# Chunk 0's gates ahead of the last attention units' closing steps, with a new place for the zero fills, the weight splits and TensorE's branch

## The reference

```python
x = x + _L0_xattn_ref(_layernorm(x), ctx, ctx, ...)   # layer norms on q, k, v, softmax, Wo; a sigmoid gate and a layer norm close it
x = x + _L0_ffn_ref(_layernorm(x), ...)               # silu(x w1) * (x w2), then gelu(h h1), gelu(h h2), h w3; ternary weights
x = x + _L1_xattn_ref(_layernorm(x), ctx, ctx, ...)   # softmax attention, w_o
x = x + _L1_ffn_ref(_layernorm(x), ...)               # relu(x W1 + b1) W2 + b2
```

## Time and profile before

| | us |
| --- | --- |
| median of 3 runs | 988.79 (988.23 to 990.15) |
| the profiled execution | 985.62 |
| its span, first to last instruction | 983.7 |
| TensorE busy | 932.3 (95%) |
| ScalarE busy | 776.5 (79%) |
| VectorE busy | 705.6 (72%) |
| GpSimd busy | 364.8 (37%) |
| mean granted TensorE clock | 0.992 |

### The profile page before, as it was taken

The page is one execution under the profiler, slowest core; times in us unless marked ns, Lnnn a source line. Parts: engine busy times, 40 slices in busy tenths (PEclk is TensorE's granted clock), DMA queues, the critical chain, the costliest instruction groups (busy, mean ns, idle before and its releaser), DMA issues.

```text
span 983.7 us, 33064 instructions
## 1 busy us (share of the span) xinstructions
PE 932.3 (95%) x12363; PEld 722.0 (73%) x12363; DVE 705.6 (72%) x1918; ACT 776.5 (79%) x1537; POOL 364.8 (37%) x546
## 2 busy tenths in 40 slices
PE   5999999999969999999999999799999999889998
PEld 3677777877658888887888887557777777558886
DVE  8789889887766666666766665366766766478985
ACT  3688888888768988888888887468878888659886
POOL 6989999997420000000000000254444443011110
PEclk9999999999999999999999999899999999999999
DMA  6333322211000000000000000022222221000111
GB/s 204 97 95 97 99 72 83 74 44 39 6 0 1 1 0 0 0 0 0 0 0 0 0 0 22 31 80 75 65 64 65 71 65 55 17 2 33 43 39 58
DMA packets 46550, 41.75 MB, mean 42 GB/s; under 512 B 24400, under 2 KB 32592, under 8 KB 46416
## 3 DMA queue, kind: packets, MB, share of 16 engines
q1 hardware_dynamic: 45408, 37.26, 12.3%
q10 hardware_dynamic: 1008, 2.64, 0.8%
HBM read 16.79 MB, written 4.19 MB: 21 GB/s over the span
## 4 chain that ended last, share of the span: by engine, by line
PE 78%; ACT 8%; DVE 6%; issue 6%; DMA 1%; POOL 0%; ACTq 0%; SPq 0%; DVEq 0%; POOLq 0%
PE ps_w L1046 15%; PE ps_w L1045 15%; PE ps_av L578 6%; PE ps_w L528 5%; ACT prob_t L671 3%; PE ps_w L525 3%; PE ps_w L511 3%; PE ps_mid L600 3%; PE ps_mid L601 3%; PE ps_turn L588 2%; PE ps_turn L615 2%; PE ps_mid L643 2%; PE p_ps_out L1044 2%; ACT v_by_head L742 2%; PE p_ps_out L1046 1%
## 5 line engine op out<-in xcount | busy, mean ns | idle before, releaser
L848 DVE TENSOR_REDUCE top<-ps_w 128x16 f32<-128x1024 f32 x128 | 155.7, 1217 | 76.6 <-PE ps_w L525 76.1
L1045 PE MATMUL ps_w<-g_h_lo,w_hi 128*128 128x512 f32 x512 | 206.1, 402 | 3.9 <-DVE g_h_lo L1266 3.9
L1046 PE MATMUL ps_w<-g_h_hi,w_hi 128*128 128x512 f32 x512 | 203.1, 397 | 0.0
L1266 DVE TENSOR_TENSOR g_h_lo<-g_h,g_h_hi 128x512 fp32r<-128x512 f32 x192 | 133.0, 693 | 91.3 <-ACT g_h_hi L1215 87.4
L133 POOL TENSOR_TENSOR front_rstd<-front_spread,minus_half 128x4 f32<-128x4 f32 x33 | 34.3, 1041 | 416.7 <-DVE front_spread L126 416.7
L525 PE MATMUL ps_w<-qk_sets,qk_t 32*64 32x256 f32 x2048 | 142.4, 387 | 0.0
L1215 ACT ACTIVATE g_h_hi<-g_h 128x512 fp32r<-128x512 f32 x192 | 121.3, 632 | 21.6 <-DVE g_h L1276 17.6
L528 PE MATMUL ps_w<-qk_sets,qk_t 32*64 32x256 f32 x2048 | 133.7, 375 | 0.8 <-issue 0.8
L671 ACT ACTIVATE prob_t<-ps_w 128x1024 f32<-128x1024 f32 x128 | 130.5, 1020 | 4.7 <-PE ps_w L528 4.5
L1045 PEld LDWEIGHTS ps_w<-g_h_lo,w_hi 128*128 128x128 f32 x512 | 96.8, 189 | 26.1 <-DVE g_h_lo L1266 4.1
L1046 PEld LDWEIGHTS ps_w<-g_h_hi,w_hi 128*128 128x128 f32 x512 | 97.0, 189 | 21.8
(11 more groups left out here) (160 smaller groups left out, 2107.4 us busy)
## 6 DMA issues: line engine op xcount, KB each, us to landing
qk_sets<-qk_t SPq DMA_DIRECT2D x256, 64.0 KB, 1.9
ctx_in<-in_ctx SPq DMA_DIRECT2D x32, 128.0 KB, 2.8
ctx_in<-in_ctx_t SPq DMA_DIRECT2D x32, 128.0 KB, 2.6
out_x<-x_res SPq DMA_DIRECT2D x16, 256.0 KB, 2.0
x_res<-in_x SPq DMA_DIRECT2D x14, 256.0 KB, 3.4
shift<-pieces SPq DMA_DIRECT2D x128, 16.0 KB, 2.3
w_raw<-in_ff_weights SPq DMA_DIRECT2D x8, 256.0 KB, 3.3
w_raw<-in_ff_weights ACTq DMA_DIRECT2D x1, 768.0 KB, 8.0
```

The lines of the kernel that those rows point to most:

```text
L848: nc.vector.tensor_reduce(out=top[:, i % 2, half, :], in_=bank_pair(half).rearrange("p (a q) -> p a q", q=SEQ), op=ALU.max, axis=AX.X).the ...
L1045: nc.tensor.matmul(out, w_hi, x_lo, start=first and w_lo is None, stop=False)
L1046: return nc.tensor.matmul(out, w_hi, x_hi, start=False, stop=last)
L1266: nc.vector.tensor_tensor(h_lo[level][:, o, :], h[:, o % 2, :], h_hi[level][:, o, :].bitcast(F32), ALU.subtract).then_inc(lo_ready[level], 1)
```

## The change

It has five parts.

1. The zero fills leave GpSimd. ScalarE fills `qk_sets` slots 0 and 1 and `v_by_head` slots 2 and 3 before its first copy, and `qk_sets` slots 2 and 3 at step -1, by copying the bf16 zeros of `blank`. VectorE's fill of `v_by_head` slots 0 and 1 moves behind unit 0's statistics. A new semaphore, `slots_cleared`, counts ScalarE's fills.
2. The four scatters of unit 0 are shared: two by SP, two by ScalarE's queue, right behind `qk_t` of unit 0.
3. `split_weights_hi` moves, in ScalarE's step, from its end to the place between `top_parts` and `top_t`.
4. VectorE's steps N+3 and N+4 of the first attention move into the gated stage: chunk 0's products first, then `front_normalise` of chunk 1 and step N+3; step N+4 ahead of chunk 1's products. For chunk 0 TensorE takes `middle(0, 1)` by quarters, waiting for one quarter at a time in its first output quarter, with the transposes of chunk 1 behind it; ScalarE's copy of these transposes follows the first gelu.
5. TensorE's three later stages are functions that are called inside both sides of the branch, so the side without low products runs on into the second attention.

The core of the diff:

```diff
@@ open_scalar
     nc.scalar.activation(t.qk_bias[:, 1, 0:1], t.cols[:, COLS["b_q"]:COLS["b_q"] + 1], ACT.Copy, scale=float(HEAD_DIM) ** -0.5)
+    act.wait_ge(op.zeros_ready, op.BLANK)
+    clear_operands(nc, t, op, slice(0, FIRST_SLOTS))
+    clear_values(nc, t, op, slice(FIRST_SLOTS, UNROLL))
@@ open_gpsimd
-    nc.gpsimd.memset(t.qk_sets[:, 0:FIRST_SLOTS, :, :, :], 0.0).then_inc(op.zeros_ready, 1)
...
-def open_late_zeros(nc, t, op):
-    late = slice(FIRST_SLOTS, UNROLL)
-    nc.gpsimd.memset(t.v_by_head[:, late, :, :], 0.0)
-    nc.gpsimd.memset(t.qk_sets[:, late, :, :, :], 0.0).then_inc(op.zeros_ready, 1)
+def clear_operands(nc, t, op, slots):
+    wide = t.qk_sets[:, slots, :, :, :].rearrange("p s m n u -> p (s m) (n u)")
+    nc.scalar.activation(wide, t.blank[:, :].unsqueeze(1).to_broadcast([P, FIRST_SLOTS * SETS, 512]), ACT.Copy).then_inc(op.slots_cleared, 1)
+
+
+def clear_values(nc, t, op, slots):
+    wide = t.v_by_head[:, slots, :, :].rearrange("p s h c -> p s (h c)")
+    width = UNIT_TILES * HEADS * PAIR_COLS
+    for s in range(FIRST_SLOTS):
+        last = nc.scalar.activation(wide[:, s, :].rearrange("p (a n) -> p a n", n=512),
+                                    t.blank[:, :].unsqueeze(1).to_broadcast([P, width // 512, 512]), ACT.Copy)
+    last.then_inc(op.slots_cleared, 1)
@@ open_values
-    nc.vector.memset(t.v_by_head[:, 0:FIRST_SLOTS, :, :], 0.0).then_inc(op.chain, 1)
@@ open_weights
     nc.vector.tensor_copy(t.qk_bias[:, 1, 1:2], c["b_k"])
+    nc.vector.memset(t.v_by_head[:, 0:FIRST_SLOTS, :, :], 0.0).then_inc(op.chain, 1)
     dve.wait_ge(op.bias_done, 1)
@@ attention, scalar step
                     last.then_inc(qk_taken, 1)
+                if i == 0:
+                    act.wait_ge(qk_taken, 1)
+                    scatter(act, 0, range(SETS // 2, SETS))
                 if j < 0:
                     take_turned(j + 3)
+                if gated and j == -1:
+                    clear_operands(nc, t, op, slice(FIRST_SLOTS, UNROLL))
...
                     nc.scalar.activation(top_parts[:, j % 2, :, :, :], each_part, ACT.Copy).then_inc(top_split, 1)
+                split_weights_hi(nc, t, t.opening, act, layer, j)
                 if on(j):
                     act.wait_ge(top_turned, j + 1)
...
                 if j >= 0:
                     take_turned(j + 3)
-                split_weights_hi(nc, t, t.opening, act, layer, j)
@@ attention, vector
-                if j == N + 3:
+                if not gated and j == N + 3:
                     front_normalise(nc, t, front, dve, 1, front.slots - 1)
...
-            for j in range(-5, N + 5):
+            t.first_attention_step = step
+            for j in range(-5, N + 3 if gated else N + 5):
@@ gated_feed_forward, tensor: middle and step
+            def middle(i, level, between=None):
...
+                by_quarter = isinstance(i, int) and (i == 0 if level == 1 else i + 1 >= N)
+                if not by_quarter:
+                    wait(pe, lo_ready[level - 1], 4 * i + 4)
...
+                        if by_quarter and o == 0:
+                            wait(pe, lo_ready[level - 1], 4 * i + c + 1)
...
+                    if o == 0 and between is not None:
+                        between()
...
+                if opening(j):
+                    middle(j, 1, between=turn_next)
+                else:
+                    turn_next()
                     middle(j, 1)
@@ gated_feed_forward, vector step
+                if opening(j):
+                    split_lo(j, 1, 0)
                 if ahead(j + 1):
                     front_split_in(nc, t, front, dve, j + 1, 0, ps_in[:, :])
...
+                if opening(j):
+                    t.first_attention_step(t.tiles // UNIT_TILES + 4)
                 product_stage(j + 1)
+                if opening(j + 1):
+                    front_normalise(nc, t, front, dve, 1, 0)
+                    t.first_attention_step(t.tiles // UNIT_TILES + 3)
                 residual(j - 1)
@@ two_layer_xattn_ffn
+            @block.tensor
+            def _(pe):
+                with pe.If(t.lows_absent):
+                    t.gated_stage(pe, with_lo=False)
+                    t.second_attention(pe)
+                    t.plain_stage(pe)
+                with pe.Else():
+                    t.gated_stage(pe, with_lo=True)
+                    t.second_attention(pe)
+                    t.plain_stage(pe)
```

More of the change, by code:

```diff
@@ L494, in attention, with scatter, tensor_program @@
         closing_row = t.ln_o_b[:, :] if gated else t.bias_row[:, 1, :]
+        def scatter(queue, i, sets):
+            s = i % UNROLL
+            for m in sets:
+                queue.dma_start(qk_sets[m:P:SETS, s, m, :, :], qk_t[m:P:SETS, i % QKT, :, :]).then_inc(qk_landed[s], 16)
         def bank_pair(half):
             return ps_w[:, half * 1024:(half + 1) * 1024]
-        @block.tensor
-        def _(pe):
+        def tensor_program(pe):
             def half_step(turned_unit, turned_half, unit, half):
@@ L664, in _ @@
                     t.lows_absent = pe.value_load(t.lo_bits_row[0:1, 0:1].bitcast(I32))
+        if gated:
+            block.tensor(tensor_program)
+        else:
+            t.second_attention = tensor_program
         @block.scalar
@@ L839, in _ @@
                 step(j)
-                if gated and j == -2:
-                    open_late_zeros(nc, t, op)
         @block.vector
@@ L1070, in following, with opening @@
         return isinstance(i, int) and i == N
+    def opening(j):
+        return isinstance(j, int) and j == 0
     LEVELS = 3
@@ L1186, in _, with hidden @@
-            with pe.If(t.lows_absent):
-                program(with_lo=False)
-            with pe.Else():
-                program(with_lo=True)
+                up(j + 1, (0, 1))
+                down(j - 1)
+                up(j + 1, (2, 3))
+                turn_back(j - 1)
+                middle(j, 2)
+            steps.run(pe, step)
+        t.gated_stage = tensor_program
         @block.scalar
         def _(act):
-            def hidden(i, level):
+            def hidden(i, level, between=None):
@@ L1196, in hidden @@
                 for o in range(4):
+                    if o == 1 and between is not None:
+                        between()
                     wait(act, done[level], 4 * i + o + 1)
@@ L1245, in step, with take_next @@
             def step(j, u):
-                if ahead(j + 1):
-                    front_take_in(nc, t, front, act, j + 1, 0, ps_in[:, :])
-                hidden(j, 1)
+                def take_next():
+                    if ahead(j + 1):
+                        front_take_in(nc, t, front, act, j + 1, 0, ps_in[:, :])
+                if opening(j):
+                    hidden(j, 1, between=take_next)
+                else:
+                    take_next()
+                    hidden(j, 1)
                 silu_stage(j + 1, after=j - 1)
@@ L1293, in step @@
                     front_measure(nc, t, front, dve, N, 0, chunk=0)
-                if on(j):
+                if on(j) and not opening(j):
                     split_lo(j, 1, 0)
```

132 lines of the change are left out of this document (61 added, 71 removed).

## The result

The changed kernel takes 975.3 us (median of four runs, 972.8 to 975.7) against 989.5 for the one before (median of four beside it, 988.2 to 991.2): a ratio of 0.985, 95% interval 0.983 to 0.986. A second series gave 973.8 against 987.5, ratio 0.986 (0.983 to 0.989). So the gain is 14.2 and 13.7 us where 13.8 was forecast.

The account below looks back on a forecast made before the run. TensorE carries 78% of the chain, so only its standstills can move. Savings of 1.7 + 3.1 + 1.0 + 4.2 + 3.8 = 13.8 us take the median from 988.8 to 975.0, range 972 to 978.

Parts of the forecast that it names:

- The opening: Start of the kernel: zero fills off GpSimd let the first values come sooner, 1.7 us gained, from -1 to 3.
- The splits: Attention steps with a weight split: the earlier w_hi copy gains 3.1 us in the first attention, 1.0 in the second.
- the allowance of 0.15 us for each split: First attention's six split steps: 0.9 us in all left as cost, taking the gain from 4.0 to 3.1.
- The first border: First attention to gated stage: first product 2.9 us earlier, level 1 ending 5.4 or 3.8 earlier, 4.2 taken.
- The wait for `front_normalise`: First border: TensorE's transposes of chunk 1 wait from two matmuls' end at 276.5 until 277.05, a new wait.
- The second border: Gated stage to second attention: without the jump's 3.09 us wait qk_t starts 3.9 us earlier, 3.8 kept.
- The next wants (unit 2's normed rows, 628.5) are met: Second border: what TensorE needs after the earlier first products is ready in time, so 3.8 us is kept.
- The jump at the end: End of TensorE's program: a 3.1 us jump ends at 983.5, inside the span; counted as nothing, 0.5 at most.
- Rival B: Second border: the wait is not the jump's, or returns as another; gain 10.0 us, time 978.8; chance 0.12.
- C: Attention: ScalarE bounds the steps, so moving its 0.63 us copy gains nothing; time 979.1; chance 0.10.
- D: Opening gives nothing, ScalarE's fills and queue issue eating VectorE's gain; -1 instead of 1.7, time 977.7; chance 0.08.
- E: ScalarE's fills run below a third of the expected pace and eat the 13.8 us gain; time 991; chance 0.02.

Follow-up runs that it names:

- split_at_end: The changed kernel with part 3 undone, the copy to w_hi back at the end of ScalarE's step: 978.9 us.
- warm: Zero matmuls added in TensorE's waits at both borders, against the kernel with shared scatters behind ScalarE's copy of transposes: 968.3 us, ratio 0.980.
- jump: The changed kernel with part 5 undone, the branch closing behind the gated stage: 979.2 us, ratio 0.991.
- fills_gpsimd: The changed kernel with ScalarE's three zero fills back on GpSimd: 975.9 us, ratio 0.988.

## Why the prediction was right, point by point

**The opening, 1.7 forecast.** The two pairs of profiles give 1.05 and 1.7 at the same row. The mechanism is the one named: `halves` at 0.39 us, ScalarE's fills hidden, the first values at 22.91 (22.5 forecast). The fills' pace was 0.88 to 0.97 ns a column for 0.8, so the fills ahead of the first copy ended at 11.65 instead of 11.1; 0.54 us of slack was left only because the first copy came at 12.20 instead of 11.8. VectorE's own fill takes 1.76 us with no fill on GpSimd beside it, as before, not the 1.2 that I took. The Trainium skill, "SBUF — State Buffer", Who interferes with whom, says that a VectorE instruction with at most one SBUF input, outside the two-port modes, does not contend with GpSimd. The trace agrees: the fill takes 1.76 us both beside GpSimd's fill and without it. The 1.2 us that I had worked out for the opening by that rule lies, like my 1.7, within what the two pairs show.

**The splits, 3.1 and 1.0 forecast.** The twelve steps gave 3.8, nearly the whole upper bound of 4.0 (4.5 in the second pair, where they took 90.45 us before): the allowance of 0.15 us for each split, 0.9 in all, was largely unneeded, since 0.25 us are left in the twelve steps. In the second attention the two split steps became 6.74 us like the others. Undoing the part costs 5.1 us. But the first attention keeps only part of it: of eleven profiles with the split moved ten show the stall near 238 us (0.2 to 1.2 us, always in the same group of value matmuls), and none of the three without the move does. The eleventh is of a program that shows it in its other profile. TensorE's own program is the same in `split_at_end` and the changed kernel, so that program alone does not decide it; what does, the runs don't show. Where the rest of the 1.7 us of the first pair went in the last steps (0.7 of the second) I did not settle.

**The first border, 4.2 forecast.** 4.3 and 3.7 in the profiles, 4.3 by undoing it. The first product follows the silu's end by 0.04 us, and the clock did fall, as I leaned to. The wait for `front_normalise` that I had put at 0.6 us did not show, because the slow clock made the matmuls ahead of it last until then; at full clock (`warm`) the transposes wait 0.29:

```profile
272.98 0.66 PE L153 MATMUL ps_turn<-ident,front_normed 128*128 128x128 f32 x4 [0.29 <-DVE front_normed L143]
```

**The second border, 3.8 forecast: the step that failed.** The jump's wait went (no idle time ahead of the fill), and the kernel without shared scatters, at full clock, shows the 3.8 as 3.8 to 4.0. What failed is "The next wants (unit 2's normed rows, 628.5) are met": I had followed part 2 in the opening only, where I wrote that ScalarE's two issues delay its copy of unit 1's transposes, and not in the second attention, where the same lines run. There TensorE waits 2.41 us for that copy, against 0.82 without sharing. A second step failed in one of the two profiles: the first queries were to run at full clock, and in the first profile they ran at 0.50, as before the change. The term was 2.7 us at full clock and 0.4 where the clock fell.

**The end of the second attention, nothing forecast.** With the branch closed ahead of it TensorE stalls twice, 0.8 to 1.3 and 0.3 to 0.5 us, at fixed instructions far behind the jump, and four steps take 2.5 us more. Part 5 removes that as well. Undone, part 5 costs 5.5 us; I had a reason for 3.8 of it and none for the 2.5 at the end of this attention, and the jump at the program's end takes a part back.

**The jump at the end, 0 forecast with 0.5 at most.** The last residual add ends 2.6 us before the span's end in the three profiles that end without a jump. In the changed kernel it is 3.3 us (here the last row of VectorE; the span is 973.7):

```profile
969.69 0.69 DVE L1480 TENSOR_TENSOR x_res<-p_ps_back,x_res 128x512 f32<-128x512 f32 x1 [0.81 <-PE p_ps_back L1431]
```

In the ten others that end with one it is 3.0 to 4.1. So the program ends 0.4 to 1.5 us later than without the jump there, where I had allowed 0.5. The Trainium skill, "Runtime: NRT & Kernel Launch", Instruction fetch mechanics, says that a taken branch outside the fetched window stops the engine for a fetch. The trace shows no row for that jump, only the later end, so it neither confirms nor refutes the fetch as the reason.

**The sum.** Undone one at a time the parts are worth 5.5 (branch), 5.1 (splits), 4.3 (border), 2.1 (fills) and -3.1 (sharing): 13.9 us, and the whole is 13.7. Each of the five is good to about 1 us and two are taken across series, so this says only that nothing large is missing, not that the parts add to a tenth. That the total came within 0.1 to 0.4 us of 13.8 is luck: a missed gain of about 2.5 us made up for a border short by 1 to 3 and for the later end. The parts that were forecast for the right reason are the opening, the splits and the first border.

Rival B said that the wait is not the jump's, or comes back at once as another. The first half is refuted by `jump`; the second came true in part, as the 2.41 us for unit 1's transposes. C is refuted by `split_at_end`, D by `fills_gpsimd` and the milestones, E by the fill rows. (E's own sum is off by one: 988.8 less 13.8 plus 15 is 990, not 991.)

## What to carry to other kernels

An edit in code that two stages share must be followed through both: two queue issues in front of a small copy cost at most a few tenths of a microsecond in the opening, where VectorE held the chain, and 1.2 us at the second border, where TensorE did. Where an engine's program closes a branch, look not only at the jump but at stalls without a releaser far behind it. And where TensorE has waits under 1 us in a row, a few matmuls on zeros in them are cheap to try, though one profile does not show that they are what keeps the clock up; of all versions here the one with scatters behind the copy and such fillers was the fastest, 968.3 us.

## What the runs showed of the hardware that I had not expected

- TensorE stalls without a releaser in the middle of straight runs of matmuls: 0.2 to 1.2 us in one group of 64 near 238 us (with 5 of them left in eight profiles, 2 in two, and no stall in the eleventh), and 0.2 to 1.4 us at places that change from one execution to the next in the second attention. What ends them was not settled.
- The granted clock at the second border was 0.57 in one execution and 1.00 in another of the same program, with the same waits ahead of it. A single profile's clock there can't carry a term of 1 to 2 us.
- ScalarE copies a broadcast row of bf16 zeros to 4096 float columns in 3.60 us, 0.88 ns a column, hardly slower than GpSimd's fill (3.51 us). VectorE's `halves`, 4.37 us beside GpSimd's fill, take 0.39 with ScalarE's fill starting 0.24 us behind them.
